# Second-layer tiles handed out chunk by chunk, and a written table of split tiles, in a two-layer graph kernel

## What is computed

```python
h = maximum(layernorm(x), 0)
hW = h @ W0 + B0
mask = (adj < 0.5) & ~eye
S = where(mask, exp(-(1/adj - 1/mu)**2 / (2*sigma**2)), 0)
x = x + S @ hW                       # layer 1
h = maximum(layernorm(x), 0)
x = x + (adj*adj + eye) @ (h @ W1.T) # layer 2
```

## Time and profile before

| | |
|---|---|
| median of 3 runs | 1870.15 us (1869.32 to 1871.13) |
| profiled execution, its own time | 1871.51 us |
| span in the trace | 1869.6 us |
| TensorE busy | 1835.1 us (98%) |
| VectorE busy | 1743.2 us (93%) |
| ScalarE busy | 1731.2 us (93%) |
| mean granted TensorE clock | 0.996 |

### The profile page before, as it was taken

One profiled execution on the slowest core, in us unless ns is written; L12 is line 12 of the kernel. 1 busy time (PEld: TensorE's weight loads), 2 busy tenths in 40 slices (PEclk: granted clock), 3 DMA queues, 4 the chain that ended last, 5 costly groups with the idle time before them and its releaser, 6 DMA issues.

```text
span 1869.6 us, 13360 instructions
## 1 busy us (share of the span) xinstructions
PE 1835.1 (98%) x4836; PEld 884.6 (47%) x4836; DVE 1743.2 (93%) x1029; ACT 1731.2 (93%) x985; POOL 96.1 (5%) x118
## 2 busy tenths in 40 slices
PE   7989999999999999999999999999999999999998
PEld 4544444444444444444444444444444444555665
DVE  7999999999999999999999998999999994778796
ACT  8999899999999999999999999999999998888664
POOL 0000000000000000000000000000000000000111
PEclk9999999999999999999999999999999999999999
DMA  8476889897978787777878776676756678866998
GB/s 315 162 288 257 319 305 308 288 324 246 330 267 316 261 298 278 276 279 275 284 263 304 237 247 241 249 255 228 255 200 232 232 265 297 291 253 229 311 339 250
DMA packets 85297, 507.29 MB, mean 271 GB/s; under 512 B 9840, under 2 KB 10480, under 8 KB 28144
## 3 DMA queue, kind: packets, MB, share of 16 engines
q1 hardware_dynamic: 69840, 476.68, 67.0%
q0 software_dynamic: 15248, 29.63, 9.2%
q10 hardware_dynamic: 144, 0.13, 0.0%
HBM read 476.51 MB, written 29.88 MB: 271 GB/s over the span
## 4 chain that ended last, share of the span: by engine, by line
PE 76%; DVE 11%; ACT 8%; issue 3%; DMA 1%; SPq 0%; DVEq 0%
PE p_x L483 21%; PE p_l1b L449 20%; PE p_l1a L449 15%; PE p_own L483 11%; DVE rings L626 4%; DVE rings L619 3%; ACT rings L801 3%; DVE rings L637 2%; ACT rings L811 2%; ACT rings L806 2%; PE p_l1a L483 1%; PE p_x L461 1%; PE p_x L462 1%; PE p_x L463 1%; PE p_own L461 1%
## 5 line engine op out<-in xcount | busy, mean ns | idle before, releaser
L619 DVE SCALAR_TENSOR_TENSOR rings<-rings 128x2048 f32<-128x2048 f32 x256 | 584.6, 2284 | 35.9 <-PE p_l1b L449 31.0
L626 DVE SCALAR_TENSOR_TENSOR rings<-rings,small 128x2048 f32<-128x2048 f32 x256 | 599.9, 2344 | 14.4 <-ACT rings L806 14.2
L811 ACT ACTIVATE rings<-rings,small 128x2048 f32<-128x2048 f32 x256 | 533.1, 2082 | 47.0 <-DVE rings L626 46.5
L801 ACT ACTIVATE rings<-rings,small 128x2048 f32<-128x2048 f32 x256 | 509.6, 1991 | 15.3 <-DVE rings L619 11.6
L483 PE MATMUL p_x<-rings,h 128*128 128x512 f32 x1144 | 513.3, 592 | 0.0
L806 ACT ACTIVATE rings<-rings 128x2048 f32<-128x2048 f32 x256 | 488.0, 1906 | 5.6
L449 PE MATMUL p_l1b<-rings,h 128*128 128x512 f32 x1024 | 461.2, 596 | 0.0
L449 PE MATMUL p_l1a<-rings,h 128*128 128x512 f32 x1024 | 458.4, 593 | 0.7 <-DVE h L687 0.7
L483 PEld LDWEIGHTS p_x<-rings,h 128*128 128x128 f32 x1144 | 216.8, 190 | 266.3 <-issue 264.8
L637 DVE TENSOR_TENSOR rings<-rings 128x2048 f32<-128x2048 f32 x136 | 310.4, 2282 | 1.6
L449 PEld LDWEIGHTS p_l1b<-rings,h 128*128 128x128 f32 x1024 | 195.2, 191 | 240.7 <-issue 237.6
(11 more groups left out here) (92 smaller groups left out, 571.0 us busy)
## 6 DMA issues: line engine op xcount, KB each, us to landing
rings<-adjT SPq DMA_DIRECT2D x446, 1024.0 KB, 6.9
outT<-xa_buf POOLq DMA_DIRECT2D x97, 256.0 KB, 7.3
x_buf<-xT SPq DMA_DIRECT2D x24, 256.0 KB, 6.4
outT<-y_buf POOLq DMA_DIRECT2D x15, 256.0 KB, 7.5
xa_buf<-xT SPq DMA_DIRECT2D x8, 256.0 KB, 5.6
outT<-x_buf POOLq DMA_DIRECT2D x1, 256.0 KB, 5.0
y_buf<-outT SPq DMA_DIRECT2D x1, 256.0 KB, 12.6
outT<-y_buf SPq DMA_DIRECT2D x1, 128.0 KB, 1.8
```

Of the source, the lines that this page charges most:

```text
L619: dve.scalar_tensor_tensor(out=tile(s_ring, slot_of(t)), in0=tile(a_ring, slot), scalar=CUTOFF, in1=tile(a_ring, slot), op0=ALU.is_lt, op1 ...
L626: dve.scalar_tensor_tensor(out=v, in0=v, scalar=neg_2c, in1=v, op0=ALU.add, op1=ALU.mult).then_inc(squared, 1)
L801: act.activation(v, v, ACT.Ln, bias=tiny_c).then_inc(ln_done, 1)
L811: act.activation(v, v, ACT.Exp, bias=exp_bias, scale=neg_k).then_inc(sens_done, 1)
```

## The change

The table of shares is written out for every chunk. The rule for splitting (`m % 7 not in (1, 4)`, 41 items) is replaced by a string with one letter for each of the 58 items that may be split: 47 are marked, 43 with `S` (VectorE makes both halves, as before) and 4 with `A` (ScalarE copies `high` right after its square, VectorE makes only `low`). The four are items 206, 215, 236 and 250. (The change's title says five; the string holds four.)

```diff
-QUOTA = [0, 11, 13] + [12] * 3 + [13] * 9
+QUOTA = [0, 11, 13, 11, 14, 12, 14, 12, 13, 13, 12, 14, 12, 12, 12]
...
-SPLITS = [it for it in ITEMS if it.step >= LAST + SPLIT_STEP.get(it.source, STEPS) and it.row != it.source
-          and it.m % 7 not in (1, 4)]
+
+MAY_SPLIT = [it for it in ITEMS if it.step >= LAST + SPLIT_STEP.get(it.source, STEPS) and it.row != it.source]
+WHICH = "SSSSSSSSSSS.SAS..SSSSASS.S.SSSSSS.S.SS.SA.SSSSS.SSS.SSASSS"
+SPLITS = [it for it, w in zip(MAY_SPLIT, WHICH) if w != "."]
+HIGH_BY = {it.m: "act" if w == "A" else "dve" for it, w in zip(MAY_SPLIT, WHICH)}
...
                 dve.wait_ge(q_by[it.by], it.squares)
-                if it.split < 3:
-                    dve.wait_ge(s_used, LAST)
-                else:
-                    dve.wait_ge(q_used, SPLITS[it.split - 3].m + 1)
-                dve.tensor_copy(high[:, :], squares).then_inc(high_ready, 1)
-                dve.wait_ge(high_ready, it.split + 1)
+                if it.high_by == "dve":
+                    if it.split < 3:
+                        dve.wait_ge(s_used, LAST)
+                    else:
+                        dve.wait_ge(q_used, SPLITS[it.split - 3].m + 1)
+                    dve.tensor_copy(high[:, :], squares).then_inc(high_by["dve"], 1)
+                dve.wait_ge(high_by[it.high_by], it.highs)
                 dve.tensor_tensor(low_ring[it.load % A_RING][:, :], squares, high[:, :].bitcast(F32),
...
                     squares.then_inc(q_by["act"], 1)
+                if it.split is not None and it.high_by == "act":
+                    act.wait_ge(q_by["act"], it.squares)
+                    act.wait_ge(q_used, SPLITS[it.split - 3].m + 1)
+                    act.activation(high_ring[it.split % 3][:, :], a, ACT.Copy).then_inc(high_by["act"], 1)
```

More of the change, by code:

```diff
@@ L177 @@
     it.split = r
+    it.high_by = HIGH_BY[it.m]
+    it.highs = len([x for x in SPLITS[:r + 1] if x.high_by == it.high_by])
 Q_COUNT = {"dve": 0, "act": 0}
@@ L317, in gnn_program @@
         q_used = sem("q_used")
-        high_ready = sem("high_ready")
+        high_by = {"dve": sem("high_by_dve"), "act": sem("high_by_act")}
         low_ready = sem("low_ready")
```

## The result

The changed kernel takes 1858.3 us (median of 6 runs, 1857.92 to 1858.78) against 1871.25 of the kernel before on the same chip: a ratio of 0.9932, 95% interval 0.9919 to 0.9945, so 13.0 us less. The span fell from 1869.6 to 1856.6 us.

A forecast was written before the change was run, and what follows sets the result against it. TensorE was taken as the bound, except VectorE in chunks 3 to 5. Terms -2.9 - 4.3 - 2.6 - 1.7 - 1.9 = -13.4, plus 1.0 for small waits, took 1870.15 to 1857.8, said as 1857.5 us; range 1853.5 to 1865.

The forecast's parts named there:

- Middle: Chunks 3 to 6: new shares cut the excess over TensorE's pace from 5.8 to 2.9 us, -2.9.
- My reason for chunk 4: Chunk 4: the 2.27 us stall goes, as the moved item precedes `centre_row` and VectorE arrives a square earlier.
- Splits: Dense chunk and tail: six more split items, each 0.71 us shorter on TensorE, -4.3 us.
- the wait at 215: Item 215, step 253: a third item removes the 2.58 us stall (-2.6) and the half-clock stretch behind it (-1.7).
- tail: Items 229 and 231 become plain, so the waits of 0.50 and 1.06 us go: -1.9 with semaphore latency.
- The allowance of 1.0 for level steps: Dense chunk: 1.0 us added for small waits, three steps being level to 0.02 us.
- ready at T + 6.17: A step's last item, both halves on VectorE, is ready 6.17 us after its layer-1 tile ends; 4.91 with `A`.
- ScalarE's copies: Four `high` copies on ScalarE, taken as 1.90 us each, finish before TensorE needs `sensitivity`: cost 0.
- VectorE misses the beat: Rival, dense chunk: VectorE's 12.0 against 12.3 us a step fails, two stalls with slow clock return 8.6: 1866, chance 0.13.
- VectorE becomes the bound: Rival, last 296 us: VectorE's extra 15.7 us go on the path, 1883 us, chance 0.05.
- Handed back in chunk 6: Rival: the gain of the new shares is lost in chunk 6, VectorE 104.5 against TensorE 102.2: 1860.5 us, chance 0.12.
- not on the path: Rival: saved matmul time isn't on the path, only stalls could go; 1868 to 1870 us, clock unmoved; chance 0.05.

## Why the prediction was right

**Middle, -2.9 forecast, -2.5 measured.** An item more beside chunk 4 was nearly free (0.9 us), with VectorE at the same load in the three windows. I had reckoned its load at 297.1 for them, 6.5 less than it was busy, and at 104.5 in chunk 6, where it was busy for 100.6. The split was off: chunk 3 is 2.8 us long where I had 1.2, chunk 4 0.5 where I had 0.2, chunks 5 and 6 nothing where I had 0.9 and 0.6. That the sum is near is partly luck. Nor was VectorE alone the bound: the new wait of 1.0 in chunk 3 is ScalarE's. My reason for chunk 4, the item ahead of `centre_row`, is only part: with that item alone the wait went, and TensorE waited 1.5 us in place of 0.6 behind it.

**Splits, -4.3; the wait at 215, -2.6 - 1.7; tail, -1.9.** Together 10.5, measured 10.9. The wait and its clock drop were shown alone (3.8 in the window for 3.6), the tail alone (2.8 for 2.6), and step 253's third item as the cause by giving it back. The 0.71 of a split was not tested alone; it is the difference of two start-to-start times. The 0.2 to 0.4 us more in each window I can't place.

**The allowance of 1.0 for level steps.** It wasn't needed: no wait for `low` is left. But the 0.3 us that VectorE was to have in hand each step were not there. The rule "ready at T + 6.17" holds only while VectorE waits at `premask`. At step 254 it is 0.40 late already, behind a wait of 0.63 for ScalarE's square, which the sum of VectorE's work alone doesn't have. What keeps item 215 in time, by 0.13, is the A marks, on 206 as on 215. By the rule I had priced them at 0.7 us (the difference of 5.44 and 6.17 at one step); taken away, they cost 5.4. The tail's slack, which I took as covered by a mean, was 0.15 to 5 us an item.

**ScalarE's copies, 0.** Right for these four: 1.92 us each (I took 1.90), one 3.1 us wait for the ring in the tail, no `sensitivity` late in the dense chunk.

**The rivals.** "VectorE misses the beat" and "VectorE becomes the bound" did not come, but were nearer than my 0.13 and 0.05 suggest: four marks removed gave back 5.4, eleven splits more cost 36. "Handed back in chunk 6" and "not on the path" are refuted by gapless windows of 102.21 and 98.77. The trace speaks against one of the Trainium skill's two measures for TensorE here (Perfetto Trace Analysis, Identifying the Most-Contended Engine): weight loads stayed at 48% while TensorE set the pace.

**The number.** 1857.5 forecast, 1858.3 measured, with two errors that partly cancel. The sum of -12.4 is 0.6 short of the 13.0. The 1.35 us that I took off, because the median of the kernel before lay that far below its profiled execution, and 0.3 of rounding had little behind them: over six runs that median is 1871.25, 0.3 below, and the changed kernel's lies 0.1 below its profiled execution.

**Left open.** What decides whether the clock falls after a wait. That ScalarE's load is behind the wait at 415.9 is read from the trace and not tested.

## What to carry to other kernels

An engine's idle share over a stretch says little about room for more work when it runs in order behind short rings: here VectorE was idle for 42 of 292 us, and 42 us of added work made the stretch 37 us longer, at most 7 of them by the clock. Follow a delay round the other engines too: the next input of a late engine may hang on its own output. Count the work between two points where it must wait, and how far the ring lets it run ahead; a slower item now and then buys the lead that a run of fast ones spends. And where an item's late half stands behind a wait, what counts is how much the waiting engine has to do in front of it, so moving a whole item into that step can be worth more than speeding the half up.

## What the runs showed of the hardware

TensorE's clock did not fall by the length of a wait alone. Waits of 2.58 (the kernel before) and 1.87 us (no A marks) were followed by 3.4 us at half of full speed; waits of 1.32 and 1.71 were not, nor was one of 2.19 in the kernel with all 58 split, nor the 2.58 at the same item in the kernel with the dense chunk as before. The wait of 2.27 in chunk 4 was followed by full clock in the kernel before and in the ones with 215 plain and with 215's copy on ScalarE, but not in the kernel with the new tail, whose instructions there are the same. Windows of 8 us from that wait on, in the kernel with 215's copy on ScalarE:

```profile
437.00:445.00 8.00, 6.63 (x16) 3.04 (x17) 7.96 (x7) 5.42 (x4) 0.86 (x1) 1.00 0.59 160
```

and in the kernel with the new tail:

```profile
438.00:446.00 8.00, 7.23 (x13) 3.15 (x14) 7.97 (x7) 5.42 (x4) 0.86 (x1) 0.79 0.46 119
```

The column ahead of the last two is the granted clock, 1.00 and 0.79. So the 1.7 us that I put on the wait at item 215 are a price that is paid in some executions and not in others: of four kernels whose profile has this wait of 2.58, three show the stretch of half clock. In chunk 4 the stretch cost nothing in sum: chunk 4's window was 0.9 us longer and chunk 5's 0.8 shorter. The first 236 us of the span differed by up to 3.4 us between kernels that are the same there, and with them the stretches of half clock at the start.
